# Another start within a 64-byte line for the matmul operands of a two-expert-layer transformer block

## What is computed

```python
x = x + 0.5 * ffn(layernorm(x))     # 8 experts, top 2 by a softmax gate
x = x + attn(layernorm(x))          # 16 heads of 16; each row sees itself and its two neighbours
x = x + 0.5 * ffn(layernorm(x))     # the same expert weights again
# ffn: gates = softmax(x @ Wg + bg); the two best, scaled to sum 1;
#      out = sum over these two of gate_e * (x @ We[e] + be[e])
# attn: xp = x @ Wp.T + bp; q, k, v = projections of xp; softmax over 3 neighbours; @ Wo.T + bo
```

## Time and profile before

| | |
|---|---|
| median of 3 runs | 1117.84 us (1116.78 to 1118.46) |
| the profiled execution | 1119.13 us |
| its span, first to last instruction | 1117.1 us |
| mean granted PE clock | 0.981 of 2.4 GHz |
| PE busy | 1055.4 us, 94% |
| DVE busy | 904.2 us, 81% |
| POOL busy | 714.0 us, 64% |
| ACT busy | 528.1 us, 47% |

### The profile page before, as it was taken

One profiled execution on the slowest core, in us unless ns is written; L12 is line 12 of the kernel. 1 busy time (PEld: TensorE's weight loads), 2 busy tenths in 40 slices (PEclk: granted clock), 3 DMA queues, 4 the chain that ended last, 5 costly groups with the idle time before them and its releaser, 6 DMA issues.

```text
span 1117.1 us, 17965 instructions
## 1 busy us (share of the span) xinstructions
PE 1055.4 (94%) x5459; PEld 884.0 (79%) x5459; DVE 904.2 (81%) x2611; ACT 528.1 (47%) x1181; POOL 714.0 (64%) x953
## 2 busy tenths in 40 slices
PE   5898699999999999999999999999999999999775
PEld 3676588888888888888888888888888888887553
DVE  3658688888888888888898888888988888888873
ACT  3264354544555554445555545455555454544331
POOL 2376366667777666667776666677766666664443
PEclk9899799999999999999999999999999999999998
DMA  5001000000000000000000000000000000000000
GB/s 165 10 28 36 14 1 20 20 20 21 20 20 20 2 19 20 20 20 20 20 20 10 10 20 20 20 20 20 20 10 10 20 20 21 10 11 10 11 11 19
DMA packets 12583, 23.05 MB, mean 21 GB/s; under 512 B 2212, under 2 KB 5812, under 8 KB 12488
## 3 DMA queue, kind: packets, MB, share of 16 engines
q1 hardware_dynamic: 9240, 13.37, 3.4%
q0 software_dynamic: 3248, 8.54, 2.7%
HBM read 12.47 MB, written 8.39 MB: 19 GB/s over the span
## 4 chain that ended last, share of the span: by engine, by line
PE 84%; DVE 6%; SPq 3%; DMA 2%; issue 2%; ACT 1%; POOL 0%; POOLq 0%; DVEq 0%; ACTq 0%
PE ffn_bank L885 19%; PE ffn_bank L887 19%; PE ffn_bank L886 19%; PE tr_bank L914 5%; PE tr_bank L926 4%; PE mix_bank L885 4%; PE mix_bank L886 4%; PE mix_bank L887 4%; SPq L243 2%; PE tr_bank L885 1%; PE tr_bank L886 1%; PE tr_bank L887 1%; PE mix_bank L951 1%; DMA we_raw<-in_L_ffn_We 1%; DMA moved_x_bo<-x_bo 1%
## 5 line engine op out<-in xcount | busy, mean ns | idle before, releaser
L885 PE MATMUL ffn_bank<-we_hi,T_hi 128*128 128x512 f32 x1024 | 414.2, 405 | 3.7 <-DVE chain_sum L656 3.2
L887 PE MATMUL ffn_bank<-we_hi,T_lo 128*128 128x512 f32 x1024 | 402.9, 393 | 0.0
L886 PE MATMUL ffn_bank<-we_lo,T_hi 128*128 128x512 f32 x1024 | 402.0, 393 | 0.0
L446 ACT ACTIVATE we_raw<-ffn_bank,gate 128x256 f32<-128x256 f32 x512 | 209.1, 473 | 139.3 <-PE ffn_bank L887 138.3
L332 POOL TENSOR_TENSOR chain_sum<-chain_sum,we_raw 128x512 f32<-128x512 f32 x128 | 165.6, 1294 | 134.1 <-DVE chain_sum L656 132.4
L885 PEld LDWEIGHTS ffn_bank<-we_hi,T_hi 128*128 128x128 f32 x1024 | 193.9, 189 | 43.1 <-DVE chain_sum L656 4.8
L887 PEld LDWEIGHTS ffn_bank<-we_hi,T_lo 128*128 128x128 f32 x1024 | 193.4, 189 | 42.7
L886 PEld LDWEIGHTS ffn_bank<-we_lo,T_hi 128*128 128x128 f32 x1024 | 194.2, 190 | 34.9
L409 ACT CAST T_hi<-tr_bank 128x512 fp32r<-128x512 f32 x128 | 74.8, 588 | 169.5 <-PE tr_bank L914 169.4
L656 DVE SCALAR_TENSOR_TENSOR chain_sum<-ffn_bank,gate,chain_sum 128x256 f32<-128x256 f32 x256 | 111.5, 476 | 46.6 <-PE ffn_bank L887 46.6
L309 POOL TENSOR_TENSOR var_eps<-mean_var,eps 128x2 f32<-128x2 f32 x96 | 20.6, 215 | 146.4 <-DVE mean_var L574 146.4
(11 more groups left out here) (126 smaller groups left out, 1831.2 us busy)
## 6 DMA issues: line engine op xcount, KB each, us to landing
out_x<-y SPq DMA_DIRECT2D x31, 256.0 KB, 2.0
we_raw<-in_L_ffn_We SPq DMA_DIRECT2D x2, 1024.0 KB, 14.6
x_in<-in_L_attn_x,x_row POOLq DMA_INDIRECT x60, 3.1
x_in<-in_L_attn_x SPq DMA_DIRECT2D x2, 256.0 KB, 7.8
moved_qk<-qk SPq DMA_DIRECT2D x4, 124.0 KB
w_raw<-in_L_attn_Wq SPq DMA_DIRECT2D x1, 256.0 KB, 2.9
w_raw<-in_L_attn_Wk SPq DMA_DIRECT2D x1, 256.0 KB, 3.0
w_raw<-in_L_attn_Wv SPq DMA_DIRECT2D x1, 256.0 KB, 5.2
```

The source lines that it names most:

```text
L446: last = nc.scalar.activation(scaled[:, f, t, half, j], ffn_bank[b][:, j * D:(j + 1) * D], ACT.Copy, scale=gate[:, 2 * f + t, e:e + 1])
L885: nc.tensor.matmul(dest, hi[:, t, k, :], w_hi_[:, k, c0:c1], start=(first and k == 0), stop=False, skip_group_check=not first)
L886: nc.tensor.matmul(dest, hi[:, t, k, :], w_lo_[:, k, c0:c1], start=False, stop=False, skip_group_check=not first)
L887: last = nc.tensor.matmul(dest, lo[:, t, k, :], w_hi_[:, k, c0:c1], start=False, stop=(k == KB - 1), skip_group_check=not first)
```

## The change

The same instructions are issued in the same order with the same waits on every engine. Only the order of the declarations changes, and two tensors of 32 bytes are added that nothing reads or writes (pad_0, pad_1). bg_all (32 bytes) now lies between we_hi and we_lo, minus_half behind we_lo, so that wqkv_hi begins at 0 again; the T tensors come behind wo_lo, in another order and with the pads among them; minus_one stands where it keeps ident at 32.

```diff
-        we_hi, we_lo = sb("we_hi", [PART, KB, E * D], f32r), sb("we_lo", [PART, KB, E * D], f32r)
+        we_hi = sb("we_hi", [PART, KB, E * D], f32r)
+        bg_all = sb("bg_all", [PART, E])
+        we_lo = sb("we_lo", [PART, KB, E * D], f32r)
+        minus_half = sb("minus_half", [PART, 2])
         wqkv_hi, wqkv_lo = sb("wqkv_hi", [PART, KB, 3 * D], f32r), sb("wqkv_lo", [PART, KB, 3 * D], f32r)
         wo_hi, wo_lo = sb("wo_hi", [PART, KB, D], f32r), sb("wo_lo", [PART, KB, D], f32r)
+        T_hi, T_lo = [None] * 4, [None] * 4
+
+        def T_part(half, i, c):
+            return sb(f"T_{half}{i}_{c}", [PART, 2, KB, PART], f32r)
+
+        hi0, lo0, hi3 = T_part("hi", TA, 0), T_part("lo", TA, 0), T_part("hi", TD, 0)
+        pad_0 = sb("pad_0", [PART, 8])
+        lo3 = T_part("lo", TD, 0)
+        T_hi[TA], T_lo[TA] = [hi0, T_part("hi", TA, 1)], [lo0, T_part("lo", TA, 1)]
+        T_hi[TB], T_lo[TB] = [T_part("hi", TB, 0)], [T_part("lo", TB, 0)]
+        T_hi[TD] = [hi3, T_part("hi", TD, 1)]
+        pad_1 = sb("pad_1", [PART, 8])
+        T_lo[TD] = [lo3, T_part("lo", TD, 1)]
+        T_hi[TO], T_lo[TO] = [T_part("hi", TO, 0)], [T_part("lo", TO, 0)]
+
         wg = sb("wg", [PART, KB, 2, E], f32r)
         be_rows = sb("be_rows", [PART, NF * 2, D], f32r)
         bqkv = sb("bqkv", [PART, 3 * D])
         bo_all = sb("bo_all", [PART, D])
-        bg_all = sb("bg_all", [PART, E])
-
+        minus_one = sb("minus_one", [PART, 2])
         ident = sb("ident", [PART, PART])
...
-        minus_half, minus_one, eps = (sb(name, [PART, 2]) for name in ("minus_half", "minus_one", "eps"))
+        eps = sb("eps", [PART, 2])
...
-        T_hi = [[sb(f"T_hi{i}_{c}", [PART, 2, KB, PART], f32r) for c in range(2 if i in (TA, TD) else 1)] for i in range(4)]
-        T_lo = [[sb(f"T_lo{i}_{c}", [PART, 2, KB, PART], f32r) for c in range(2 if i in (TA, TD) else 1)] for i in range(4)]
```

## The result

The changed kernel takes 1121.63 us (median of 6 runs, 1120.91 to 1123.03), the kernel before 1117.75 us beside it; the ratio is 1.0042, with a 95% interval of 1.003 to 1.0054. It is slower by 3.9 us where no change was forecast. The time lies within the stated range of 1109 to 1127 us, and outside the 1116 to 1120 us of the forecast alone. A ratio here is the record's estimate from the single runs, not the quotient of the two medians (1.0035 here); the two differ by up to 0.0014. A second set of runs, with the kernel before beside it again, gave 1122.83 against 1117.47 us, ratio 1.0043 (1.003 to 1.0056).

What follows compares the result with a forecast made beforehand. TensorE, busy throughout 160 to 960 us, was taken as the bound; 2304 matmuls times x, with x = 0, and 0 for the other engines left 1117.8 us. The stated range was 1109 to 1127 us.

Steps and rivals of the forecast that it cites:

- The bound: TensorE is busy all the time from 160 to 960 us, so any later or earlier matmul start moves the end.
- there is nothing for it to wait for: Claim that TensorE, busy 800.00 of 800.00 us from 160 to 960 us, waits for nothing there.
- x = 0: Extra time per matmul with moved operands, taken as 0 for 2304 matmuls; ends kept were -7 and +4.4 ns.
- gateT with be_rows: Four matmuls loading gateT from 32 beside be_rows streaming from 0: 117.5 ns each, difference 0 from everything at 0.
- The count of pairs: Expert matmuls whose moving operand and load beside it come to differ in 64-byte-line half: 1536 of 3072.
- streams that don't settle: Slower rival: TA's 1536 expert matmuls stay at the after-break pace, +4.4 ns each, 6.8 us, 1124.6 us; slower in all 0.29.
- Its argument against itself: Against the slower rival: after four gateT loads TensorE is back at 227 ns some four matmuls later.
- reads that get out of each other's way: Faster rival: different line halves give back part of the 13 ns surcharge, 1920 x 4 ns = 7.7 us, 1110 us; chance 0.24.
- The remark on the 215.8 ns: Skill page's figure for 512 columns, 11 ns below the trace; freeing that in 1920 matmuls would give 1097 us.

Runs made afterwards that it cites:

- all32: Kernel before with 32 bytes of padding ahead of the first tensor, so all tensors move 32 bytes and keep their distances; ratio 1.0003.
- T192: Kernel before with the block of all twelve T tensors moved by 192 bytes; 1112.62 against 1115.88 us, ratio 0.9963.
- probe1: Kernel before with 72 settings of 36 matmuls appended, varying the places of stream and load; 512 columns took 227 ns with both at 0, 233 with the load at 32.
- probe2: Kernel before with a second set of settings appended, 24 matmuls each, mostly behind four transposes; 256 columns took 120, 114 and 118 ns with the load at 0, 64, 192.
- lo32: Kernel before with only we_lo moved, by 32 bytes, other tensors keeping their places modulo 512; 1121.87 against 1115.26 us, ratio 1.0049.
- halves256: Kernel before with the change's 32-byte shifts, but weights and T tensors otherwise a multiple of 256 bytes apart, not 64; ratio 1.0065.

## Why the prediction was wrong

**The bound held in the main.** PE is busy in all of the 800 us before and after, and the count of matmuls there moves as the time does: 4212 and 4213 in the kernels with ratios 1.0065 and 1.0063, 4221 in the changed one, 4247 in the kernel before and in all32, 4259 in T192. But "there is nothing for it to wait for" was read from the bars and is not so. PE waited some 80 ns for ScalarE's normed in each step, and of the time by which its matmuls start later 1.7 us over 24 steps did not move the end.

**The step that failed is x = 0,** the price of a matmul whose operands are moved. The expert matmuls measured +2.5 to +4.3 ns. The zero was taken "by the row that is nearest to the case, gateT with be_rows". That row was no witness, for three reasons that the runs showed. Both sides of the comparison stood behind a break, before a stream had settled; what the change destroys is the settled pace, and the prediction compared two unsettled ones. It had 256 columns, where in the probes places that don't agree are mostly faster (117 to 119 ns against 120), not slower, as they are with 512; its own two places are 32 bytes apart modulo 256. And it was four matmuls long. The sum needed x = +2.5 to +4.3 ns, and for all expert matmuls; the rows of this trace had no stream of 512 columns with places that differ, so its sign could not be had from them, and the row should have been given less weight.

**The count of pairs failed as well.** I reduced each place to a half of a 64-byte line, because the change speaks of one. In the kernel before all places of L885 to L887 agree modulo 256 bytes; in the changed kernel the T block is 64 bytes off that, besides the shifts by 32. By halves TD slot 0 was to stay at 227 ns and 1536 expert matmuls were to be touched; modulo 256 none of the sets keeps its place, and all four lost the pace (+2.5 ns in TD slot 0, +4.3 in TA slot 0). TO, which I counted as untouched, changed too: 120.2 to 118.3 ns. The declarations give all starts in bytes and so showed this before any run.

**The rival that came true** is the first, streams that don't settle, in its mechanism and in part of its size. Its price of 4.4 ns, from the step behind a break, is what the sets lost at most. Its number of matmuls was wrong (1536 by halves, where 3072 are affected at 2.5 to 4.3 ns): 7.5 us over 24 steps instead of 6.8 us over all. At the rate of the 24 steps all 3072 would make 10 us. The result is less for several reasons: PE's wait ahead of TD shrinks by 1.7 us over 24 steps and 256 columns gain 0.8 us, which leaves 5.35 us there; the 768 expert matmuls outside lengthen nothing; and in the first profile that outer part was 3 us shorter, at a higher granted clock. So that the price of 6.8 us comes near the 3.9 and 5.4 us by which the medians differ is in part luck. Its argument against itself, that PE was back at 227 ns after gateT, was no argument: places that agree settle again after any upset, and in the changed kernel they don't agree.

**The other rival**, reads that get out of each other's way, is false for 512 columns and true for 256, which the prediction did not think to separate. At the best places the surcharge is 13.3 ns for 320, 384, 448 and 512 columns alike (146.7 - 133.3, 173.3 - 160.0, 200.0 - 186.7, 226.7 - 213.3) and more for 496 and 508 (16.6 and 15.0), and only with 256 columns did a stream go below it, to 113.3 ns.

**The remark on the 215.8 ns** of the Trainium skill (TensorE: Matmul & The Clock Gate, section Back-to-back issue gap) changed nothing. These runs don't agree with it: the shortest steady pace of 512 columns in any setting of both probes is 226.6 ns.

## What to carry to other kernels

Where TensorE streams without a gap, look at the byte addresses of its moving and stationary operands, not only at their order: in this kernel, with 512 columns of float32r, all of them equal modulo 256 bytes (and at a multiple of 32) gave 226.7 ns a matmul and nearly anything else 228 to 238, while 256 columns wanted another distance (192 bytes: 113.3 instead of 120 ns in the kernel, 117.8 in the probes) and 448 columns did too. An inserted tensor of 32 bytes moves everything behind it, so two versions of a kernel should be compared with the places of the operands kept, by padding. Count the matmuls in a stretch in which PE is always busy, or better take the time of a fixed number of equal steps; it shows half a percent in one profile, without the noise of filling and draining (764.02 us twice, in the kernel before and in all32, and 769.37 and 769.35 in the two profiles of the changed kernel).

## What the hardware showed that was not expected

- The pace of equal matmuls depends on the places of stream and load with a period of 256 bytes (to within 1.6 ns; probe1 and probe2), from 226.6 to 237.8 ns for 512 columns. Why 256, and why 240 bytes is as good as 256 when the stream is at 0 (226.7 ns) and not when it is at 32, 64 or 128 (228.3 ns), was not settled; memory banks would be a guess, and no run shows them.
- At the lower clock (1.2 GHz) nothing of it is seen, whatever the places: 256 columns start every 213.3 ns in the kernel before, in the changed one, in lo32, halves256 and T192, and 512 columns every 426.6 to 427 ns before and in the second profile of the change. In the changed kernel, with stream and load 32 bytes apart, seven steps take 1.49 us:

```profile
118.23 0.41 PE L903 MATMUL mix_bank<-wqkv_hi,T_lo 128*128 128x256 f32 x1
...
119.72 0.41 PE L901 MATMUL tr_bank<-wo_hi,T_hi 128*128 128x256 f32 x1
```

- The same places can have two steady paces, 117.8 and 113.3 ns for 256 columns 64 bytes apart.
- One operand of three at another place slows another matmul than its own too (lo32: 6.9 ns on its own, 2.9 on one of the two others), and neither the load beside the stream nor the operand in the array alone decides.
